# Cross-attention and mixture of experts: the bias of the exponential on GpSimd, the second half of the scores one unit later

## What is computed

```python
q = (layernorm(x) @ Wq + bq)            # 16 heads of 32
k, v = split(ctx @ Wkv + bkv)
q = fq_sym(q / sqrt(32), axis=head_dim) # s = max|q|/127, at least 1e-8; round(q/s)*s
k = fq_sym(k, axis=head_dim)
v = fq_sym(v, axis=keys)
a = softmax(q @ k.T)                    # 2048 x 2048 for each of 16 heads
a = fq_unsigned(a, axis=-1)             # s = max(a)/255; round(a/s)*s
x = x + (a @ v) @ Wp + bp
x = x + experts(layernorm(x))           # top 4 of 32 experts and a shared one
```

## Time and profile before

| | us |
|---|---|
| median of 3 runs | 1729.8 (1724.31 to 1731.87) |
| the profiled execution | 1726.54 |
| its span | 1724.3 |
| PE, DVE busy over the span | 75%, 61% |
| ACT, POOL busy over the span | 49%, 47% |
| granted TensorE clock, mean | 0.88 |

### The profile page before, as it was taken

How to read it: one execution, slowest core, us unless ns; L and a number is a source line. 1 busy time by engine, 2 the same in 40 slices (tenths; PEclk the granted TensorE clock), 3 DMA queues, 4 the chain that set the end, 5 groups by cost and what they waited for, 6 DMA issues and landing times.

```text
span 1724.3 us, 27234 instructions
## 1 busy us (share of the span) xinstructions
PE 1295.8 (75%) x7762; PEld 657.0 (38%) x7858; DVE 1060.4 (61%) x1895; ACT 850.3 (49%) x1186; POOL 814.0 (47%) x746
## 2 busy tenths in 40 slices
PE   8997777777877777777774143999999999999300
PEld 3443233444444444444432011544445444454100
DVE  5455999999999999999994701323233232333344
ACT  2223898889998988999893000222222222222000
POOL 0002577777777777777773274021212212121465
PEclk9998798888898989999886576999999999999755
DMA  8553465655555555555552321489999999999576
GB/s 251 141 130 89 93 121 114 129 126 134 128 127 116 128 116 124 126 127 128 104 127 59 141 79 37 133 304 350 362 364 355 365 353 365 358 362 358 182 236 216
DMA packets 404788, 330.14 MB, mean 191 GB/s; under 512 B 347779, under 2 KB 347907, under 8 KB 393988
## 3 DMA queue, kind: packets, MB, share of 16 engines
q1 hardware_dynamic: 391172, 291.76, 57.1%
q0 software_dynamic: 13568, 37.79, 7.0%
HBM read 199.37 MB, written 46.22 MB: 142 GB/s over the span
## 4 chain that ended last, share of the span: by engine, by line
PE 39%; issue 25%; DVE 24%; POOL 3%; ACT 3%; DMA 2%; another core or an unknown queue 2%; DVEq 1%; POOLq 0%; SPq 0%; ACTq 0%
PE psS L942 18%; DVE mem L525 14%; PE psS L952 9%; DVE mem L555 3%; POOL mem L1048 3%; PE psS L419 2%; PE psS L1359 2%; PE psAV L390 2%; PE psAV L932 1%; PE psP L913 1%; PE psT L913 1%; DMA mem<-y_dram,mem 1%; PE psP L1340 1%; DVE mem L1063 1%
## 5 line engine op out<-in xcount | busy, mean ns | idle before, releaser
L610 POOL TENSOR_SCALAR mem<-mem 128x2048 bf16<-128x2048 uint8 x256 | 485.5, 1901 | 174.1 <-DMA mem<-mem 166.9
L478 ACT ACTIVATE mem<-mem 128x2048 uint8<-128x2048 f32 x256 | 536.1, 2094 | 12.4
L419 PE MATMUL psS<-mem 128*128 128x512 bf16 x929 | 324.0, 426 | 174.5 <-DVE mem L555 125.8
L942 PE MATMUL psS<-mem 128*128 128x512 f32 x768 | 352.7, 601 | 0.0
L555 DVE TENSOR_SCALAR_CACHE_REDUCE mem<-psS,mem 128x1024 f32<-128x1024 f32 x256 | 328.1, 1282 | 25.5 <-DVE mem L525 2.7
L525 DVE TENSOR_SCALAR_CACHE_REDUCE mem<-psS 128x1024 f32<-128x1024 f32 x256 | 311.7, 1217 | 13.0 <-PE psS L419 12.8
L991 DVE TENSOR_SCALAR mem<-psS 128x512 f32<-128x512 f32 x96 | 66.4, 692 | 361.2 <-PE psS L942 299.5
L899 POOL DMA_INDIRECT mem<-xn_dram,mem x80 | 78.4, 980 | 349.8 <-PE psT L913 171.1
L983 ACT ACTIVATE mem<-mem 128x256 f32<-128x256 f32 x96 | 40.1, 417 | 362.0 <-DVE mem L991 335.3
L952 PE MATMUL psS<-mem 128*128 128x512 f32 x384 | 184.5, 603 | 28.6 <-ACT mem L978 28.6
L942 PEld LDWEIGHTS psS<-mem 128*128 128x128 f32 x768 | 140.8, 193 | 142.9 <-issue 142.9
(11 more groups left out here) (184 smaller groups left out, 1275.2 us busy)
## 6 DMA issues: line engine op xcount, KB each, us to landing
mem<-in_moe_w SPq DMA_DIRECT2D x84, 1536.0 KB
y_dram<-mem SPq DMA_DIRECT2D x96, 256.0 KB
mem<-in_x SPq DMA_DIRECT2D x32, 256.0 KB, 2.8
y_dram<-mem SPq DMA_DIRECT2D x16, 512.0 KB, 3.7
mem<-mem SPq DMA_TRANSPOSE x288, 2.8
mem<-in_ctx_in SPq DMA_DIRECT2D x16, 256.0 KB, 3.3
x_dram<-mem SPq DMA_DIRECT2D x16, 256.0 KB, 2.2
xn_dram<-mem SPq DMA_DIRECT2D x16, 256.0 KB, 2.1
```

The source lines that it names most:

```text
L419: last = nc.tensor.matmul(psS[c][:, k * D:(k + 1) * D], qT[p][:, h, :], kT[:, h, c * HALF + k * D:c * HALF + (k + 1) * D], start=True, sto ...
L478: nc.scalar.activation(p8[slot], S[slot], ACT.Exp, bias=NB[:, slot:slot + 1], scale=sq[p][:, h:h + 1], accum_out=Z[p][:, h:h + 1]).then_in ...
L610: nc.gpsimd.tensor_scalar(pb[slot], pT[slot].bitcast(U8).rearrange("p (j q b) -> p j b q", b=2, q=P), 1.0, 0.0, ALU.mult, ALU.add).then_in ...
L942: last = nc.tensor.matmul(bankG[l % 2], xT[l % 2][:, c, :], w1[:, c, :], start=(c == 0), stop=(c == DC - 1))
```

## The change

In words:

1. The bias of the exponential leaves ACT. POOL makes it (L607 in the new file) at the head of its step n: it waits for the unit's second maximum (`half_max[1]`) and, from the fifth unit on, for the exponential four units earlier. The constant tile `ln255` goes.
2. PE's step n makes the first half of unit n and the second half of unit n-1. DVE's step n copies the first half of unit n and then the second half of unit n-1.
3. `BEHIND` is 3: POOL's step n makes the bias of unit n and then converts unit n-3. `LAG` stays at 6, `NS` at 4.
4. The query scale: the operation against 1e-8 becomes one with two tensor inputs (`least`, a tile of 1e-8), and the factor L505 goes, since the rounding takes `QSCALE` itself.
5. `pool_spread` writes three copies instead of four. The fourth quarter of `qst` is zeroed once at the start.
6. ACT's copy of the attention's transposes goes from h = 8 to h = 7; PE's projections go from h = 9, 11, 13, 14 to 9, 10, 12, 14; the router's pieces and its copy one head later.

```diff
-    BEHIND = 2
-    OUT_AT = (9, 11, 13, 14)
+    BEHIND = 3
+    OUT_AT = (9, 10, 12, 14)
...
-            if there(t):
-                scores(1)
+            if within(n - 1):
+                scores(1, n - 1, p if h else 1 - p, (h - 1) % H)
...
-                nc.scalar.activation(NB[:, slot:slot + 1], M[:, 2 * slot + 1:2 * slot + 2], ACT.Identity,
-                                         bias=ln255[:], scale=nsq[p][:, h:h + 1]).then_inc(bias_ready, 1)
...
-            nc.vector.tensor_scalar(sq[p], amax, QSCALE / 127.0, 1e-8, ALU.mult, ALU.max).then_inc(q_scale, 1)
+            nc.vector.scalar_tensor_tensor(sq[p], amax, QSCALE / 127.0, least, ALU.mult, ALU.max).then_inc(q_scale, 1)
...
-            nc.vector.tensor_scalar(rz2, rc, QSCALE, None, ALU.mult).then_inc(q_factor, 1)
...
-            nc.vector.tensor_tensor(hv(q8), hv(psP[:]), bc(rz2, HD), ALU.mult).then_inc(q8_ready, 1)
+            nc.vector.scalar_tensor_tensor(hv(q8), hv(psP[:]), QSCALE, bc(rc, HD), ALU.mult, ALU.mult).then_inc(q8_ready, 1)
...
+            if within(n - 1):
+                dve.wait_ge(scores_made[1], n)
+                dve.wait_ge(half_max[0], n)
...
-            nc.gpsimd.tensor_scalar(qst, hv(q8).unsqueeze(2).to_broadcast([P, H, 4, HD]),
+            nc.gpsimd.tensor_scalar(qst[:, :, 0:3, :], hv(q8).unsqueeze(2).to_broadcast([P, H, 3, HD]),
                                         1.0, 0.0, ALU.mult, ALU.add).then_inc(q_spread, 1)
...
+            if there(t):
+                slot = l % NS
+                if h == 0:
+                    pool.wait_ge(minus_ready, t + 1)
+                    apart(pool, t + 1)
+                pool.wait_ge(half_max[1], n + 1)
+                apart(pool, n + 1)
+                if due(n - NS + 1):
+                    pool.wait_ge(exp_done, n - NS + 1)
+                    apart(pool, n - NS + 1)
+                nc.gpsimd.tensor_scalar(NB[:, slot:slot + 1], M[:, 2 * slot + 1:2 * slot + 2],
+                                            nsq[p][:, h:h + 1], LN255, ALU.mult, ALU.add).then_inc(bias_ready, 1)
```

More of the change, by code:

```diff
@@ L243, in attention_and_experts @@
         q_amax = sem("q_amax")
-        q_factor = sem("q_factor")
+        least_ready = sem("least_ready")
         q_recip = sem("q_recip")
@@ L334, in there, with within @@
             return not isinstance(t, int) or 0 <= t < TT
+        def within(n):
+            return not isinstance(n, int) or 0 <= n < TT * H
         block = es.enter_context(nc.Block())
@@ L413, in pe_step, with scores @@
             t = 2 * tt + p
-            def scores(c):
-                if due(n):
-                    pe.wait_ge(half_max[c], n)
+            def scores(c, m, pm, hm):
+                if due(m):
+                    pe.wait_ge(half_max[c], m)
                 for k in range(HALF // D):
-                    last = nc.tensor.matmul(psS[c][:, k * D:(k + 1) * D], qT[p][:, h, :],
-                                            kT[:, h, c * HALF + k * D:c * HALF + (k + 1) * D],
+                    last = nc.tensor.matmul(psS[c][:, k * D:(k + 1) * D], qT[pm][:, hm, :],
+                                            kT[:, hm, c * HALF + k * D:c * HALF + (k + 1) * D],
                                             start=True, stop=True)
@@ L426, in pe_step @@
                     pe.wait_ge(queries_moved[p], 16 * (tt + 1))
-                scores(0)
+                scores(0, n, p, h)
             if not isinstance(n, int) or 0 <= n - LAG < TT * H:
@@ L446, in pe_step @@
                 pe_finish(pe, t - 1, 1 + OUT_AT.index(h), psAV[1 - p])
-            if h == 10:
+            if h == 11:
                 pe_route(pe, t - 2, 0)
-            if h == 12:
+            if h == 13:
                 pe_route(pe, t - 2, 1)
@@ L461, in act_step @@
                 nc.scalar.activation(xnT.rearrange("p c t -> p (c t)"), psT[:], ACT.Copy).then_inc(query_ev, 1)
-            if h == 8 and there(t - 1):
+            if h == 7 and there(t - 1):
                 if due(t):
@@ L519, in dve_step @@
             t = 2 * tt + p
-            slot = l % NS
+            slot, before = l % NS, (l - 1) % NS
             if there(t):
@@ L551, in dve_step @@
                 dve_mean(dve, 1, t - 2)
[L552 to L557, removed]
+            if within(n - 1):
+                dve.wait_ge(scores_made[1], n)
+                dve.wait_ge(half_max[0], n)
+                nc.vector.tensor_scalar(S[before][:, HALF:TK], psS[1][:], 1.0, M[:, 2 * before:2 * before + 1],
+                                            ALU.mult, ALU.max,
+                                            accum_out=M[:, 2 * before + 1:2 * before + 2]).then_inc(half_max[1], 1)
+            if h == 14 and there(t - 2):
                 if due(t - 1):
@@ L1156, in _ @@
             nc.gpsimd.memset(neghalf[:], -0.5).then_inc(constants_ready, 1)
-            nc.gpsimd.memset(ln255[:], LN255).then_inc(ln255_ready, 1)
+            nc.gpsimd.memset(least, 1e-8).then_inc(least_ready, 1)
+            nc.gpsimd.memset(qst[:, :, 3, :], 0.0).then_inc(least_ready, 1)
             nc.gpsimd.memset(ones3[:], 1.0).then_inc(constants_ready, 1)
@@ L1175, in _ @@
                 nc.gpsimd.tensor_scalar(vTb[:, m, :], vT8[:, m, :], 1.0, 0.0, ALU.mult, ALU.add).then_inc(v_whole, 1)
+            pool.wait_ge(least_ready, 2)
             pool_spread(pool, 0, 0)
@@ L1305, in _ @@
                 nc.vector.tensor_scalar(vT8[:, m, :], vT[:, m, :], rv[:, m:m + 1], None, ALU.mult).then_inc(v8_ready, 1)
+            dve.wait_ge(least_ready, 1)
             dve_scale(dve, 0, 0)
```

11 lines of the change are left out of this document (2 added, 9 removed).

## The result

| | us |
|---|---|
| before, median of 4 | 1730.3 (1724.3 to 1731.9) |
| changed, median of 4 | 1775.2 (1771.2 to 1778.9) |
| ratio | 1.0265, 95% interval 1.023 to 1.030 |
| profiled execution, before and changed | 1726.5 and 1771.2 |
| attention, from the first copy of a first half to the last copy of a second | 737.3 and 780.7 |

The change makes the kernel slower by 2.65%. Nearly the whole of it, 43.4 of the 44.7 us between the profiled executions, lies in the attention. The forecast was +24 us; the time is inside the range and some 20 us above the forecast.

A forecast was written before the change was run, and what follows sets the result against it. DVE was taken to bound the attention, 2.57 us a unit. DVE's gain -49, POOL's stretch from h = 14 to 3 +49, spread +18, clock +6: +24 on 1726.5, 1750.5 us, as median 1754; range 1725 to 1786.

The forecast's parts named there:

- ring of two steps: Attention, DVE to POOL to PE to DVE: 5.0 us against 4.7 for two DVE steps, so no slack.

The follow-up runs named there:

- e6: Changed kernel with the bias back on ACT, BEHIND = 2 and the queries' DMA at h = 10 instead of 11: ratio 0.9888 to the kernel before.
- e8: Kernel before with the new query scale and three copies alone: ratio 0.9929 to the kernel before.
- e7: Kernel before with the bias on POOL and BEHIND = 3 alone, halves in the old order: ratio 1.0100 to the kernel before.

## What to carry to other kernels

When one stage of a software pipeline is taken a unit later, list everything that stands in the queue of each engine that it delays, copies and DMAs for other purposes too, and move each with it; here the split alone cost 3%, and with ACT's copy and the queries' DMA moved it gained a little (e6 against e8). An operation moved to an engine with idle time is only free if the operations behind it there aren't waited for: POOL was idle for a quarter of the attention before (busy 559 of 738 us), but the bias tied its conversions to DVE and closed a ring of two steps with no slack. Count the steps between an operation that is waited for and its consumer, and compare the ring's sum with that many of the bound's steps, before and after.

## What the runs showed of the hardware

A small VectorE operation between SBUF tiles, 128x16 and 0.17 us by itself, ended with POOL's running conversion in both forms, with one tensor input and with two; mostly it was over 0.02 to 0.03 us behind the conversion's end, so it had waited for the whole rest of it. Its median went from 0.57 us to 1.75 us (e7) without any change to it, once POOL's operation was released by VectorE and so had mostly just started. And a VectorE copy whose scalar comes from the accumulator of the copy just before it starts 1.36 us after that one; where another copy lies between the two, a copy follows the one in front of it after 1.15 us, which is 39 us over some 180 such places.
